# Attention: the next batch's layer norm in the last pair of heads, its transposes between the output tiles, projection ahead of the values, and the maxima transposed one step later

## What is computed

```python
h = _layernorm(x, axis=-1) * (1 + ca) + sa        # ca, sa: one vector for each batch
x = x + ga * _L0_attn_ref(h, Wqkv, bqkv, Wo, bo)

# _L0_attn_ref: 16 heads of 32
kqv = x @ Wqkv + bqkv
scores = jnp.einsum('bsnh,btnh->bnst', k, q) / math.sqrt(HEAD_SIZE)
scores = jnp.triu(scores) + -10000.0 * jnp.tril(ones, k=-1)
attn = jax.nn.softmax(scores, axis=2)
out = jnp.einsum('bnkq,bknh->bqnh', attn, v)
return out @ Wo + bo
```

## Time and profile before

| | |
|---|---|
| median of 3 runs | 2349.17 us (2347.24 to 2351.19) |
| the profiled execution's own time, its span | 2338.48 us, 2336.7 us |
| PE, DVE, ACT, POOL busy (share of the span) | 81%, 52%, 35%, 31% |
| mean granted TensorE clock | 0.917 of full speed |
| first `scores` of the four batches at | 125.2, 469.2, 813.2, 1155.7 us |
| first `output` of the four batches at | 364.1, 708.4, 1051.1, 1394.6 us |

### The profile page before, as it was taken

How to read it: one execution, slowest core, us unless ns; L and a number is a source line. 1 busy time by engine, 2 the same in 40 slices (tenths; PEclk the granted TensorE clock), 3 DMA queues, 4 the chain that set the end, 5 groups by cost and what they waited for, 6 DMA issues and landing times. The chain is left out here.

```text
span 2336.7 us, 35643 instructions
## 1 busy us (share of the span) xinstructions
PE 1888.4 (81%) x9947; PEld 1191.3 (51%) x9948; DVE 1212.8 (52%) x3037; ACT 821.9 (35%) x1373; POOL 723.5 (31%) x807
## 2 busy tenths in 40 slices
PE   4888887898886888877888885899999956999910
PEld 0654433654433644434644432677777745888800
DVE  3455553445544346543345644755555534665558
ACT  1345452245552244552245451222222203545500
POOL 0201115201116101126011123544444569450055
PEclk8889998899998899998799997999999977999955
DMA  6222113222203222303222305122222147654488
GB/s 207 65 55 50 40 39 101 55 55 55 55 19 101 55 55 55 73 1 101 55 55 55 73 1 198 55 100 89 95 96 86 55 144 261 220 185 152 144 306 323
DMA packets 104975, 232.54 MB, mean 100 GB/s; under 512 B 20440, under 2 KB 20440, under 8 KB 104812
## 3 DMA queue, kind: packets, MB, share of 16 engines
q1 hardware_dynamic: 81008, 171.86, 25.6%
q0 software_dynamic: 14848, 50.34, 6.1%
q10 hardware_dynamic: 8960, 8.41, 1.2%
HBM read 113.06 MB, written 67.17 MB: 77 GB/s over the span
## 5 line engine op out<-in xcount | busy, mean ns | idle before, releaser
L328 POOL TENSOR_SCALAR_AFFINE_SELECT pr<-pr 128x256 f32<-128x256 f32 x256 | 103.4, 409 | 972.1 <-ACT pr L402 972.1
L402 ACT ACTIVATE pr<-sc 128x1024 f32<-128x1024 f32 (+3 forms) x384 | 307.6, 810 | 263.7 <-PE sc L641 261.9
L661 PE MATMUL O<-pr,V 128*32 128x512 f32 (+3 forms) x3072 | 327.0, 499 | 42.4 <-ACT oD L414 42.4
L504 DVE TENSOR_REDUCE mx<-ring 128x1 f32<-128x512 f32 x256 | 169.6, 678 | 246.8 <-PE ring L616 245.0
L500 DVE CUSTOM_DVE_ANT_0 ring<-ring,mask 128x512 f32<-128x512 f32 (+3 forms) x512 | 240.7, 511 | 62.5 <-PE ring L616 60.3
L641 PE MATMUL sc<-stk 128*128 128x512 f32 (+3 forms) x768 | 241.9, 397 | 22.8 <-ACT pr L402 20.8
L641 PEld LDWEIGHTS sc<-stk 128*128 128x128 f32 x768 | 115.8, 189 | 262.7 <-ACT pr L402 157.4
L616 PE MATMUL ring<-stk 96*128 96x512 f32 (+3 forms) x768 | 218.5, 389 | 19.9 <-DMA stk<-st 13.1
L616 PEld LDWEIGHTS ring<-stk 96*128 96x128 f32 x768 | 145.5, 205 | 67.9 <-DVE mx L500 17.6
L529 DVE RECIPROCAL oD<-oD 128x128 f32<-128x128 f32 x128 | 117.6, 934 | 94.6 <-ACT oD L414 94.6
L661 PEld LDWEIGHTS O<-pr,V 128*32 128x32 f32 x3072 | 61.3, 108 | 137.1 <-issue 101.0
(11 more groups left out here) (246 smaller groups left out, 3775.2 us busy)
## 6 DMA issues: line engine op xcount, KB each, us to landing
stk<-st SPq DMA_DIRECT2D x192, 256.0 KB, 5.0
x_e<-xs SPq DMA_DIRECT2D x79, 256.0 KB, 2.6
ys<-y_e SPq DMA_DIRECT2D x79, 256.0 KB, 2.0
oT<-in_L_attn_x_dram ACTq DMA_DIRECT2D x16, 512.0 KB, 6.1
st<-in_L_attn_x_dram SPq DMA_DIRECT2D x32, 256.0 KB, 3.4
x1d<-pr SPq DMA_DIRECT2D x32, 256.0 KB, 2.1
xb<-x1d SPq DMA_DIRECT2D x32, 256.0 KB, 3.0
part<-y_sh SPq DMA_DIRECT2D x32, 256.0 KB, 2.0
```

The lines of the kernel that those rows point to most:

```text
L402: nc.scalar.activation(pr[:, g % PRB, :, off:], sc[g % 2][:, :, off:], ACT.Exp, scale=SCALE).then_inc(exp_done, 1)
L504: nc.vector.tensor_reduce(mx[:, heads[0]:heads[-1] + 1, qt, part], bank[:, 0:len(heads) * w].rearrange("p (e k) -> p e k", e=len(heads)), ...
L661: last = nc.tensor.matmul(O[row:row + 32, off:], V[:, col:col + DH], pr[:, g % PRB, e, off:], start=(i == 0), stop=(i == 4 * c + 3))
```

## The change

1. `MT_AT` becomes M_STEPS + 1: in each pair `m_transpose`, `m_rows` and `mt_evac` of the next pair stand at step 10 instead of 9.
2. `xt` gets the memory of `hlo` instead of `oT`. ACT issues the next batch's 12 loads ahead of the exponentials of pair 5 (`load_rows`), DVE runs the whole layer norm (`layer_norm`) behind the `m_rows` of pair 6, ahead of the reciprocals of pair 7, and POOL's `ln_rstd` stands around the masks of pair 7.
3. Each `output` tile is followed by the transposes of one tile of the next batch, ACT's scaling (`h_evac`) and DVE's `split`, which makes `hhi` and now `hlo` too; `h` moves to another buffer than `u`.
4. A batch begins with `project(b, 0, ...)`, and all eight `values` follow it. The first batch's layer norm, transposes and splits stand ahead of the loop; the loop has three passes, and the last batch is written out behind it.

```diff
-    V_LAG = 3
-    MT_AT = M_STEPS
+    MT_AT = M_STEPS + 1
-    ring = []
-    for j in range(NT):
-        ring.append("hT")
-        if j >= V_LAG:
-            ring.append("v")
-    ring += ["p"] * 4 + ["v"] * V_LAG + ["m"] * NM + ["mt"] * 2
+    ring = ["p"] * 4 + ["v"] * NT + ["m"] * NM + ["mt"] * 2
...
-    ring += ["w"] * NT
+    ring += ["w", "hT"] * NT
...
-        hlo = sb("hlo", [P, KC, S], f32r)
+        with nc.sbuf_tensor("xt", [P, NT, D], f32) as xt:
+            pass
+        hlo = sb("hlo", [P, NT, KC, P], f32r)
...
-        xt = oT[:, :, :].rearrange("p k s -> p (k s)").rearrange("p (j d) -> p j d", d=D)
-        h = u.rearrange("p a (k t) -> p a k t", k=KC)
+        h = pr[:, 1, :, :].rearrange("p a (k t) -> p a k t", k=KC)
# GpSimd
+            def batch(b, more):
                 for p in range(NPAIR):
-                    for s in DIAG:
+                    if more and p == NPAIR - 1:
+                        for j in range(NT // 2):
+                            ln_rstd(b + 1, j)
+                    for n, s in enumerate(DIAG):
                         upper_off(b, p, s)
...
+                        if more and p == NPAIR - 1 and n < NT // 2:
+                            ln_rstd(b + 1, NT // 2 + n)
+                normalise(b, NPAIR - 2)
+                normalise(b, NPAIR - 1)
# ScalarE
+            def h_evac(f, bank, j):
+                if j == 0:
+                    act.wait_ge(mod_in, f * 128 + 128)
+                act.wait_ge(t_done, f * NT + j + 1)
+                if j >= 2:
+                    act.wait_ge(hlo_ready, f * NT + j - 1)
+                for k in range(KC):
+                    last = nc.scalar.activation(h[:, j % 2, k, :], bank[:, k * P:(k + 1) * P], ACT.Identity,
+                                                scale=mod_t[:, 1, k:k + 1], bias=mod_t[:, 0, k:k + 1])
+                last.then_inc(h_ready, 1)
+            def batch(b, more):
+                p_evac(b, 0, range(4))
                 for j in range(NT):
...
                     v_evac(b, j)
                 mt_evac(b, 0)
                 for p in range(NPAIR):
+                    if more and p == NPAIR - 3:
+                        load_rows(b + 1)
...
                 o_copy(b, 2 * NPAIR - 1)
+                if more:
+                    for j in range(NT):
+                        h_evac(b + 1, rb[ring_at("hT", j) % 3], j)
# VectorE
+            def split(f, j):
+                dve.wait_ge(h_ready, f * NT + j + 1)
                 nc.vector.tensor_copy(hhi[:, :, j * P:(j + 1) * P], h[:, j % 2, :, :]).then_inc(hhi_ready, 1)
+                dve.wait_ge(hhi_ready, f * NT + j + 1)
+                nc.vector.tensor_tensor(hlo[:, j, :, :], h[:, j % 2, :, :], hhi[:, :, j * P:(j + 1) * P].bitcast(f32),
+                                        ALU.subtract).then_inc(hlo_ready, 1)
...
+                if more:
+                    layer_norm(b + 1)
                 for n in (NPAIR - 2, NPAIR - 1):
                     o_recip(b, n, range(RPC))
...
                     nc.vector.tensor_tensor(u[:, j % 2, :], bank[:, :], ga_bc[:, :], ALU.mult).then_inc(u_ready, 1)
+                    if more:
+                        split(b + 1, j)
# TensorE
+            def batch(b, more):
+                project(b, 0, range(4))
                 for j in range(NT):
-                    transposes(b, j)
-                    if j >= V_LAG:
-                        values(b, j - V_LAG)
-                project(b, 0, range(4))
-
-                for j in range(NT - V_LAG, NT):
                     values(b, j)
...
                 for j in range(NT):
-                    output(b, j)
+                    output(b, j, more)
+                    if more:
+                        transposes(b + 1, bank_for(b, "hT", j), j)
```

More of the change, by code:

```diff
@@ L362, in _ @@
                     nc.gpsimd.tensor_tensor(u[:, j % 2, :], u[:, j % 2, :], xr[:, j % 2, :], ALU.add).then_inc(x1_ready, 1)
+            for j in range(NT):
+                ln_rstd(0, j)
+            with pool.Fori(0, NB - 1) as b:
+                batch(b, True)
+            batch(NB - 1, False)
         @block.scalar
@@ L458, in _ @@
                 o_copy(b, 2 * NPAIR - 1)
+                if more:
+                    for j in range(NT):
+                        h_evac(b + 1, rb[ring_at("hT", j) % 3], j)
+            load_rows(0)
+            for j in range(NT):
+                h_evac(0, rb[ring_at("hT", j) % 3], j)
+            with act.Fori(0, NB - 1) as b:
+                batch(b, True)
+            batch(NB - 1, False)
         @block.vector
@@ L566, in _, with bank_for @@
                     nc.vector.tensor_tensor(u[:, j % 2, :], bank[:, :], ga_bc[:, :], ALU.mult).then_inc(u_ready, 1)
+                    if more:
+                        split(b + 1, j)
+            layer_norm(0)
+            for j in range(NT):
+                split(0, j)
+            with dve.Fori(0, NB - 1) as b:
+                batch(b, True)
+            batch(NB - 1, False)
         @block.tensor
         def _(pe):
-            def bank_for(b, kind, n):
+            def bank_for(b, kind, n, more=True):
                 at = ring_at(kind, n)
@@ L575, in bank_for, with transposes @@
                     pe.wait_ge(u_ready, b * NT + PRIMED)
+                    pe.wait_ge(h_ready, b * NT + NT)
                 else:
-                    before = ring[at - 3]
-                    primed = PRIMED if freed[before] in (h_ready, u_ready) else 0
-                    pe.wait_ge(freed[before], b * TOTAL[before] + positions[before].index(at - 3) + 1 + primed)
+                    old = at - 3
+                    while ring[old] == "hT" and not more:
+                        old -= 3
+                    before = ring[old]
+                    done = b * TOTAL[before] + positions[before].index(old) + 1
+                    if before == "hT":
+                        pe.wait_ge(h_ready, done + NT)
+                    elif before == "w":
+                        pe.wait_ge(u_ready, done + PRIMED)
+                    else:
+                        pe.wait_ge(freed[before], done)
                 return rb[at % 3]
-            def transposes(b, j):
-                bank = bank_for(b, "hT", j)
-                pe.wait_ge(xn_ready, b * NT + j + 1)
+            def transposes(f, bank, j):
+                pe.wait_ge(xn_ready, f * NT + j + 1)
                 for k in range(KC):
@@ L663, in weighted, with output @@
                 last.then_inc(pv_done, 1)
-            def output(b, j):
-                bank = bank_for(b, "w", j)
+            def output(b, j, more):
+                bank = bank_for(b, "w", j, more)
                 pe.wait_ge(o_norm, b * 8 + 7 + j // (NT // 2) + PRIMED)
@@ L705, in _ @@
                 for j in range(NT):
-                    output(b, j)
+                    output(b, j, more)
+                    if more:
+                        transposes(b + 1, bank_for(b, "hT", j), j)
+            for j in range(NT):
+                if j >= 3:
+                    pe.wait_ge(h_ready, j - 2)
+                transposes(0, rb[ring_at("hT", j) % 3], j)
+            with pe.Fori(0, NB - 1) as b:
+                batch(b, True)
+            batch(NB - 1, False)
 def apart(eng):
```

80 lines of the change are left out of this document (24 added, 56 removed).

## The result

The changed kernel takes 2296.52 us (median of 4 runs, 2291.83 to 2298.3) against 2348.49 us before (4 runs): 0.9775 of the time, 95% interval 0.9762 to 0.9788, which is 52.0 us less. The forecast was 78 less, 2271 us.

The account below looks back on a forecast made before the run. Bound: TensorE's waits (three repeating kinds, 98.1 us) and the passages between batches (88.4 us). Terms -31.6 - 6.2 - 9.2 + 17.1 - 56.4 + 8.3 = -78.0 us from 2349.2 give 2271 us; range 2248 to 2302.

Parts of the forecast that it names:

- the second rival: Ends of pairs give half: an unseen wait replaces those removed, 23 us less gain, 2294 us; chance 0.15.
- 28 ends of pairs: With the maxima one step later, the next pair starts at 4.35 instead of 6.98 us after step 9's scores.
- lost at the start of nine odd pairs without loads: Behind pairs 0, 2 and 4 the stack lands no earlier, so these nine keep only 6.2 us of gain.
- lost in three pairs 5 with loads: Load issues on ScalarE make TensorE 4.0 us later, plus 1.7 for half clock: 3 x 5.7 = 17.1 us lost.
- three passages to the next batch: From output start to the next batch's maxima: 69.6 us instead of 88.2 to 88.4, 3 x 18.8 = 56.4 us gained.
- first batch: Values no longer fill TensorE during the layer norm; maxima at 116.8 instead of 108.57 us, 8.3 us lost.
- The step that failed: Behind pairs 0, 2 and 4 the needed stack lands no earlier, leaving 0.24 to 1.00 us each, 9.0 together.
- The loads' hold: Twelve load issues in pair 5 hold ScalarE's queue 7.0 us between exponentials, bounds 5.4 to 7.4.
- The first rival: The loads hide in ScalarE's idle time in pair 5; the 17.1 and lost 2.8 come back, 2252 us; chance 0.12.
- The third rival: GpSimd's adds block Vector's splits: 4 us a passage, 1.3 at its end, layer norm 0.8 late; 2289 us; chance 0.17.
- The fourth and fifth rival: The maxima's step does nothing, 2318 us (0.03); or TensorE at half clock from pair 5 until output, 2451 us (0.03).
- One of the signs of being wrong: Half clock in pairs 6 and 7 was listed among the signs that would show the forecast wrong.

Follow-up runs that it names:

- e5: Changed kernel with eight matmuls that nobody reads ahead of TensorE's wait for the stack in pairs 1, 3 and 5: 2280.12 us, 0.9706 of before.
- e6: Changed kernel with SyncE's second group of stack DMAs (for pair p+3) held back by three steps: 2278.10 us, 0.9695 of before.
- e1: Kernel before with only MT_AT one step later, none of the rest of the change: 2325.10 us, 0.9894 of before.
- e4: Changed kernel with the even pairs' four projection banks at steps 0, 1, 2, 4 instead of 0, 2, 4, 6: 2278.35 us, 0.9702 of before.
- e7: Changed kernel with the twelve loads on SyncE and the projection banks at steps 0, 2, 4, 5: 2225.76 us, 0.9478 of before.
- e3: Changed kernel with the next batch's twelve loads issued by SyncE behind pair 7's stack DMAs, not by ScalarE: 2276.23 us, 0.968 of before.

## Why the prediction was right, and where it was off

The direction and the range held, and so did the mechanisms at the ends of the pairs and between the batches; the forecast was half as large again as what came, because of the starts of the odd pairs. That the time fell inside the range is in part luck: the upper end came from the second rival, whose size came without its mechanism. Its terms against what the trace shows:

| us | predicted | measured |
|---|---|---|
| 28 ends of pairs, 2.63 each (2.3 behind pair 6) | -72.3 | -73.4 (28 x 2.62) |
| lost at the start of nine odd pairs without loads | +17.5 | +43.4 (sum 244.5, less 9 x 22.34) |
| lost in three pairs 5 with loads | +25.0 | +32.7 (sum 99.7, less 3 x 22.34) |
| three passages to the next batch | -56.4 | -58.0 |
| first batch | +8.3 | +4.3 |
| attention | -78.0 | -49.7 |

(The prediction gives rows two and three as gains that are left: 17.5 is 9 x 2.63 - 6.2, and 25.0 is 17.1 and the 3 x 2.63 of those pairs. The measured passages and the first batch are taken to the next batch's first `scores`. To its first maxima, as the prediction counts, they are -56.1 and +5.0, and the maxima then take 0.5 to 0.7 us less in each batch. The measured terms add up to -51.0; the 1.3 between that and the last row is not placed.)

**The step that failed** is "So only 0.2 is left there. The same reading at all twelve gives 0.24 to 1.00". It saw that the stack would be late and priced the lateness with the landing times of before and at full clock. Both assumptions failed:

- The clock, put at nothing in these nine pairs. The prediction added a half-clock stretch of 1.7 us for the stall in pair 5 because "a wait of 3.25 us was followed by half clock", and none for the waits of 1.5 to 2.4 us here. They were 1.9 to 3.2, and each of these nine pairs had 3.4 to 10.2 us at half clock. e5 shows the cause: with TensorE kept busy the clock stayed up in all nine. (The row it started from is not a clean one: in the changed kernel the same maxima of pair 0 are granted 0.50 from 443.5 to 460.4 us with no wait for a stack ahead of them.)
- The landing. The pair ends sooner, and with it the second group of stack DMAs (for pair p+3, released by the pair's last scores) starts sooner: 2.2 us after the last issue of the group that is waited for, where it was 4.0 before, so that more of that group is still to land. In pair 0 of the first batch the last DMA of the group needed takes 6.6 us from its issue at 163.56, where the earlier trace rows had 5.8; over the twelve it is 5.3 to 6.6. e6 shows it: with the second group held, the nine start their maxima 4.7 us earlier.

The two can be told apart pair by pair, since at full clock a pair exceeds 22.34 us by what its maxima are late, to 0.1 us (e1, e5). In the nine pairs the maxima start 24.2 us late in sum, where the prediction had 17.5; the other 19.2 of the 43.4 us are the clock, where it had nothing. The 1.7 us for one stretch was about right: the pairs with 3.4 us at half clock lost 1.5 to 1.6 by it, those with 6.8 lost 2.4 to 2.7, and the one with 10.2 lost 3.8. e4 and e7 show that lateness and clock are all of it: with the stack there in time, odd pairs are 22.3 us.

**The loads' hold.** The bounds given for it, 5.4 to 7.4 us, did not hold 10.3 to 10.6. They came from rows where the same DMAs were issued with no stack DMAs in flight; e6 measures 5.8 to 5.9 for the case that the bounds described. These pairs also had 10.2 us at half clock, where one stretch of 1.7 us was priced. The first rival (the loads hide; its terms give 2251 us, not 2252) is refuted. The Trainium skill (DMA: Bandwidth & Descriptors, "Issuing engines are not separate DMA queues") calls the time in which a sequencer initiates a DMA usually small relative to the DMA itself. For one DMA the trace does not speak against that (the issues of `mod_t` took 0.4 to 1.3 us in the first batch, and 2.8 to 5.1 us passed until each had landed), but twelve in a row are 10.5 us on an engine that TensorE waits for. By the same section, issuing on another engine saves only that sequencer's time; e3, which does this, saves 20.3 us in three batches.

**The second rival** (ends give half, 2294 us) is what came in size, but not by its mechanism: nothing took the place of the removed waits at the ends; all of it was at the next pair's start. It named "the first bank of the next pair's maxima" among the places, which is where it was.

**The third rival** (Vector against GpSimd) was right about the instructions and wrong about the path. DVE in the last two tiles of the output:

```profile
398.63 1.10 DVE L486 CAST hhi<-pr 128x512 fp32r<-128x512 f32 x1 [0.59 <-ACT pr L432]
399.77 1.64 DVE L488 TENSOR_TENSOR hlo<-pr,hhi 128x512 fp32r<-128x512 f32 x1
...
402.51 1.13 DVE L486 CAST hhi<-pr 128x512 fp32r<-128x512 f32 x1 [0.49 <-ACT pr L432]
403.67 0.69 DVE L488 TENSOR_TENSOR hlo<-pr,hhi 128x512 fp32r<-128x512 f32 x1
```

Beside GpSimd's adds (398.19 to 400.86, and 402.09 to 403.35) the cast takes 1.1 us against 0.43, and the subtraction 1.64 against 0.69 when GpSimd is done. The rule of the Trainium skill (SBUF — State Buffer, "Who interferes with whom"), that a Vector instruction with two SBUF inputs or in a two-port mode contends with GpSimd for a shared pair of ports, fits these rows. But a tile still comes every 3.87 us, TensorE's own time, since Vector had the room. Only the tail is longer, 3.68 us instead of the 3.1 estimated.

**The passage, the layer norm and the first batch.** 70.2 us against 69.6 predicted, and the layer norm hidden with 1.74 us to spare against 1.6. The first batch's maxima start at 113.6 us instead of the 116.8 estimated, 5.0 us later than before: statistics and normalising went at 1.3 us a tile instead of 1.45, scaling at 1.4 instead of 1.5, and its projections start at 78.4 instead of 80.4.

**The fourth and fifth rival** did not come: the step gave 23.5 us alone, and half clock in pair 5 ended within 10.2 us. One of the signs of being wrong did come, without a cost: pair 7 of the first three batches had 3.4 us at half clock near its end, behind a wait of 1.41 us for a copied sum, and was 21.4 to 21.5 us long, as before.

What stays open is what decides between like waits: the clock fell behind one of 1.85 us and not behind another of 1.84 (e1), and behind two of 1.62 and 1.65 but not behind one of 1.68 (e6). Open, too, is why e7's even pairs are 0.3 us shorter.

## What to carry to other kernels

When a change makes a stage shorter, look at what the next stage reads: a transfer that is started at a fixed step of the shortened stage comes late by the gain less the slack that it had, and that part is had only if its producer moves up too (one constant here, worth 50 us with the loads on SyncE). Price a new wait of TensorE at its length and, from rows like these, the half-clock stretch that can follow it, even when the wait is under 2 us. Put DMA issues on a queue that nobody waits for; on ScalarE between exponentials they cost their full issue time, and that time was longer while other DMAs were in flight.

## What the runs showed of the hardware

- The time that an engine spends issuing DMAs depends on what else is in flight: six issues took 7.26 us beside a group of stack DMAs from another queue, and 3.03 us with that group held back (e6).
- In the four kernels that wait for a stack in odd pairs and do nothing meanwhile (after, e1, e3, e6), 42 such pairs have no loads on ScalarE. Their waits are 1.62 to 3.17 us, and the clock fell behind 40 of them (not behind 1.68 us in e6 and 1.84 in e1). In e7 it did not fall behind two waits of 0.78 and 0.83 us. One stretch of 3.4 us at half clock cost 1.44 us between two pairs with like waits.
- Eight matmuls of no use, 2.00 us long, ahead of the wait kept the clock at 1.00 in all nine pairs in which only the stack was waited for (e5), though up to 1.47 us of waiting was left behind them, and made the kernel 16.4 us faster.
- DMAs that keep the 16 engines 71% to 77% busy through a pair (e3, e7) did not lengthen that pair by anything measurable: 25.89 us beside 25.97 (pair 3 of the same batch) in e3, and 22.34 beside 22.34 (pair 1) in e7.
